# Wider runs in the second pass of a two-layer graph kernel, and its small loads, stores and finals moved to other queues and places

## The reference

```
Ax = A @ x                                            # layer 0, A = adj
x  = layernorm(x + 1.0 - 0.1*x - 0.01*sum(x*Ax, 1))
h  = x                                                # layer 1, adj without its diagonal
support = concat((adj>0)@h, (adj<0)@h)
edge    = gru_cell(support, h, w_ih_e, w_hh_e, ...)
hw      = h @ W
att     = softmax over each row of the logits that adj's signs choose
node    = gru_cell((att*adj) @ hw, h, w_ih_n, w_hh_n, ...)
x  = layernorm(h + diag(adj)*edge + diag(adj)*node)
```

## Time and profile before

| | us |
|---|---|
| median of 3 runs | 1680.99 |
| lowest, highest of them | 1678.02, 1808.76 |
| profiled execution, its own time | 1673.49 |
| its span, first to last instruction | 1671.7 |
| PE, DVE, ACT, POOL busy | 1445.0, 1368.0, 1163.8, 178.0 |

### The profile page before, as it was taken

How to read it: one execution, slowest core, us unless ns; L and a number is a source line. 1 busy time by engine, 2 the same in 40 slices (tenths; PEclk the granted TensorE clock), 3 DMA queues, 4 the chain that set the end, 5 groups by cost and what they waited for, 6 DMA issues and landing times.

```text
span 1671.7 us, 22680 instructions
## 1 busy us (share of the span) xinstructions
PE 1445.0 (86%) x6262; PEld 794.9 (48%) x6262; DVE 1368.0 (82%) x1335; ACT 1163.8 (70%) x1409; POOL 178.0 (11%) x226
## 2 busy tenths in 40 slices
PE   7987878887888888558998899899999899999995
PEld 6655656555555555224444444444444444444442
DVE  5999899898989898647878877887788788778874
ACT  6987979797979797436666666666566666666662
POOL 2000000000001010201101111110111011111100
PEclk9999999999999999779999999999999999999996
DMA  9999999999999999999999999999999999999980
GB/s 264 418 421 422 410 422 409 421 410 421 411 421 413 419 413 419 233 200 333 303 288 306 292 293 296 308 288 291 299 305 298 299 302 295 297 300 310 293 215 11
DMA packets 366090, 550.18 MB, mean 329 GB/s; under 512 B 71024, under 2 KB 333184, under 8 KB 333296
## 3 DMA queue, kind: packets, MB, share of 16 engines
q1 hardware_dynamic: 190672, 408.49, 70.5%
q10 hardware_dynamic: 174976, 141.05, 33.1%
q0 software_dynamic: 416, 0.36, 0.1%
HBM read 545.66 MB, written 4.19 MB: 329 GB/s over the span
## 4 chain that ended last, share of the span: by engine, by line
DMA 30%; issue 21%; ACTq 15%; DVE 15%; PE 9%; ACT 7%; SPq 2%; DVEq 1%; POOL 0%; POOLq 0%
DMA ring<-in_adj 18%; ACTq L247 12%; DMA h_rows<-final 11%; DVE at L806 7%; DVE ps L610 5%; ACT mask L932 5%; PE ps L572 5%; SPq L247 2%; PE ps L1033 2%; ACTq L950 1%; PE ps L539 1%; ACTq L946 1%; PE ps L1045 1%; ACTq L989 0%; ACT final L970 0%
## 5 line engine op out<-in xcount | busy, mean ns | idle before, releaser
L932 ACT ACTIVATE mask<-at 128x2048 fp32r<-128x2048 uint32 x256 | 489.4, 1913 | 281.2 <-DVE at L806 189.6
L572 PE MATMUL ps<-mask,parts 128*128 128x512 f32 x2048 | 552.0, 413 | 101.9 <-DVE ps L610 68.2
L610 DVE SCALAR_TENSOR_TENSOR ps<-ring,ps 128x2048 f32<-128x2048 f32 x256 | 584.3, 2301 | 55.3 <-PE ps L572 34.8
L806 DVE STREAM_TRANSPOSE at<-ring 128x2048 f32<-128x2048 f32 x256 | 577.8, 2290 | 43.6 <-POOL ring L719 37.9
L1033 PE MATMUL ps<-at,hk 128*64 128x512 f32 x2048 | 495.6, 620 | 79.7 <-DVE final L813 42.3
L506 ACT ACTIVATE at<-ring 128x2048 bf16<-128x2048 f32 x256 | 488.7, 1909 | 97.0 <-DMA ring<-in_adj 52.5
L572 PEld LDWEIGHTS ps<-mask,parts 128*128 128x128 f32 x2048 | 374.9, 193 | 278.8 <-DVE ps L610 203.8
L1033 PEld LDWEIGHTS ps<-at,hk 128*64 128x64 f32 x2048 | 148.7, 141 | 346.1 <-issue 250.8
L1045 PE MATMUL ps<-mask,parts 128*128 128x512 f32 x1024 | 270.2, 405 | 13.6 <-ACT final L959 12.9
L1045 PEld LDWEIGHTS ps<-mask,parts 128*128 128x128 f32 x1024 | 182.1, 188 | 152.1 <-issue 73.4
L719 POOL TENSOR_TENSOR ring<-ring,not_diag 128x256 f32<-128x256 f32 x128 | 93.8, 733 | 715.0 <-DMA ring<-in_adj 715.0
(11 more groups left out here) (152 smaller groups left out, 645.4 us busy)
## 6 DMA issues: line engine op xcount, KB each, us to landing
ring<-in_adj SPq DMA_DIRECT2D x256, 1024.0 KB, 16.2
ring<-in_adj SPq DMA_DIRECT2D x264, 512.0 KB, 10.7
ring<-in_adj ACTq DMA_DIRECT2D x248, 512.0 KB, 14.3
stage<-h_rows ACTq DMA_DIRECT2D x16, 128.0 KB, 16.3
nat<-h_rows ACTq DMA_DIRECT2D x16, 128.0 KB, 15.8
out<-final ACTq DMA_DIRECT2D x16, 128.0 KB, 15.4
h_rows<-final ACTq DMA_DIRECT2D x7, 256.0 KB, 22.7
hk<-h_rows ACTq DMA_DIRECT2D x7, 256.0 KB, 23.9
```

The lines of the kernel that those rows point to most:

```text
L572: last = nc.tensor.matmul(ps[:, 4 * (n % 2) + i, :], pair[:, t % 2, e, :], x2[:, cols], start=e == 0, stop=e == 1)
L610: nc.vector.scalar_tensor_tensor(out=gram, in0=ring[:, i % RING, :], scalar=1.0, in1=gram, op0=ALU.mult, op1=ALU.mult, accum_out=flat[:, b ...
L806: nc.vector.transpose(b["at"][:, half % 4, :, :].rearrange("p c (f q) -> p f c q", q=Q), raw[:, :, HC * part:HC * part + HC, :]).then_inc( ...
L932: nc.scalar.activation(b["mask"][:, half % MS, :, :].rearrange("p c i -> p (c i)"), b["at"][:, half % 4, :, :].rearrange("p c i -> p (c i) ...
```

## The change

- **Units.** UC goes from 8 to 16 and a unit takes 256 rows (`RH` = 8 row groups of 32) by 512 columns of each quarter. It is still 2 MB, in runs of 2 KB. Two units side by side in rows (`v` even and odd) feed four halves. A half is now 8 chunks by 256 rows; a turn fills half of the rows of a *pair* of buffers (`pair_view`), and `sign` goes over the same half. PE's weigh and add therefore wait for both halves of their pair, and a turn waits for the weighs and signs of the whole pair two before. A slot comes free after halves 2 and 3 of every four (`freed`), and is used again five halves later.
- **h loaded once a block.** `nat` is gone. POOL loads `stage` (`rows`) behind the first `no_diagonal` of the next block, and `residual` adds from it too.
- **Output.** SP stores it, behind the fifth load of the block after the next one.
- **Weighed sum.** ACT copies both parts out of ACC_T (`weighed_copies`); DVE's `weighed_sum` adds two tiles of SBUF. The first weigh waits for the two copies alone.
- **Finals.** Most steps stand one or two halves later (the tables below); `probabilities` is a step by itself; `variance` stands behind the last turn of a block and `result` in front of the second turn of the next one; `turn_h` goes to PE's third pair, behind `small`.
- **Seam.** Of the first four units SP loads quarters 0 and 1, ACT quarters 2 and 3 (`first_unit`). The norm of the eighth group stands as a whole in front of the first turn; POOL takes its power first, then stores the rows and loads them back on its own queue. ACT makes the high part of both halves of h (`high`), POOL the low part of the first (`first_low`). In the first pass `rows_back` stands four strips later.

```diff
-    UC = 8
-    U = C // UC
+    UC = 16
     SLOTS = 4
-    HC = UC // 2
+    HC = 4
+    RH = BANK // Q // 2
+    U = 2 * (C // UC)
...
+def load_unit(eng, b, prefix, k, v, groups=(0, 1, 2, 3)):
+    RH, UC, GQ, slot = b["RH"], b["UC"], b["GQ"], v % b["SLOTS"]
+    wide, rows = v // 2, v % 2
...
+def freed(v):
+    return 4 * (v // 2) + v % 2 - 5
...
+def pair_view(t, pair):
+    at = 2 * (pair % 2)
+    return t[:, at:at + 2, :, :].rearrange("p s c i -> p (s c) i")
...
-            load_unit(sp, b, "f_", 0, u)
+            load_unit(sp, b, "f_", 0, u, (0, 1))
...
-            if grp and i == 20:
-                rows_back(act, b, grp - 1)
+            if grp and i == 24:
+                act.wait_ge(b["s_scr"], 16 * grp)
+                rows_back(act, b, grp - 1, b["s_hk"][(grp - 1) % 2])
+            done = unit - (GROUPS * self.UNITS - RING)
+            if done in (3, 5, 7):
+                self.first_unit(act, done // 2 - 1)
+        self.first_unit(act, b["SLOTS"] - 1)
...
+    def first_unit(self, act, u):
+        strips = self.UNITS * self.b["GROUPS"] - self.b["RING"] + 2 * (u + 1)
+        act.wait_ge(self.s["signs_summed"], strips)
+        act.wait_ge(self.s["gram_free"], 2 + strips)
+        load_unit(act, self.b, "f_", 0, u, (2, 3))
...
+        def block(k, first, old):
+            for u in range(slots if first else 0, U):
+                sp.wait_ge(s["turned"], k * (2 * U) + freed(u))
                 load_unit(sp, b, "f_", k, u, (0, 1))
+                if old is not None and u == slots:
+                    store(old)
...
+        def rows(k):
+            pool.wait_ge(s["rows_used"], k + 1)
+            pool.dma_start(b["stage"][:, :, :], b["scratch"][bass.ds(k * BANK, BANK), :].rearrange(
+                "(b p) d -> p b d", p=P)).then_inc(s["staged_loaded"], 16)
+        def block(k, prev):
             for u in range(self.U):
                 no_diagonal(nc, pool, b, "f_", k, u).then_inc(s["diagonal_out"], 1)
+                if prev is None and u == 0:
+                    self.first.first_low(pool)
+                if prev is None and u == 1:
+                    pool.wait_ge(b["s_scr_last"], 16)
+                    rows_back(pool, b, last, b["s_hk_last"])
+                if prev is not None and u == 0:
+                    rows(prev)
+        self.first.last_power(pool)
+        store_rows(pool, b, self.first.s["ln_done"], last, b["s_scr_last"])
+        block(0, None)
...
         with pool.Fori(1, self.K) as k:
-            block(k, False)
+            block(k, k - 1)
             power(k - 1)
...
             if not (first and half < 4):
-                dve.wait_ge(s["weighed_done"], n - 3)
-                dve.wait_ge(s["mask_ready"], n - 3)
+                dve.wait_ge(s["weighed_done"], n - rows - 2)
+                dve.wait_ge(s["mask_ready"], n - rows - 2)
...
-            dve.wait_ge(s["weighed_low_copied"], k + 1)
-            nc.vector.tensor_tensor(out=wsum[hi, :], in0=ps[hi, ACC_T, :], in1=lows[hi, :],
+            dve.wait_ge(s["weighed_copied"], 2 * k + 2)
+            nc.vector.tensor_tensor(out=wsum[hi, :], in0=wsum[hi, :], in1=lows[hi, :],
...
-        AT = {3: (weighed_sum,), 4: (added_sum,), 6: (softmax, probabilities), 8: (scale,), 10: (reset,), 11: (update,),
-              14: (residual,), 15: (variance,), 16: (result,)}
-        SEAM = {1: self.first.last_mean, 2: self.first.last_variance, 3: self.first.last_rows, 8: self.first.second_low}
+        AT = {4: (added_sum,), 5: (weighed_sum,), 6: (softmax,), 7: (probabilities,), 10: (scale,), 12: (reset,),
+              13: (update,), 15: (residual,), 16: (variance,)}
+        SEAM = {0: (self.first.last_mean, self.first.last_variance, self.first.last_rows), 8: (self.first.second_low,)}
...
+                if old is not None and half == 1:
+                    result(old)
...
-                act.wait_ge(s["added_done"], n - MS + 1)
+                act.wait_ge(s["added_done"], n - half % 2 - 2)
...
-            u = half // 2 + SLOTS
-            if half % 2 == 1 and (u < U or not last):
+            u = 2 * (half // 4 + 2) + half % 2
+            if half % 4 >= 2 and (u < U or not last):
                 load_unit(act, b, "f_", k + u // U, u % U, (2, 3))
...
-            nc.scalar.copy(b["lows"][hi, :], ps[lo, ACC_T, :]).then_inc(s["weighed_low_copied"], 1)
+            nc.scalar.copy(b["lows"][hi, :], ps[lo, ACC_T, :]).then_inc(s["weighed_copied"], 1)
+            nc.scalar.copy(b["wsum"][0][hi, :], ps[hi, ACC_T, :]).then_inc(s["weighed_copied"], 1)
...
-        AT = {1: (weighed_low, rows), 2: (added_low,), 5: (exps,), 6: (state_in,), 9: (gates,), 10: (new,), 16: (store,)}
+        AT = {1: (weighed_copies,), 2: (added_low,), 6: (exps,), 7: (state_in,), 11: (gates,), 12: (new,)}
...
-                pe.wait_ge(s["weighed_low_copied"], k)
-                pe.wait_ge(s["weighed_summed"], k)
+                pe.wait_ge(s["weighed_copied"], 2 * k)
...
-            pe.wait_ge(s["turned"], k * H + half + 1)
+            pe.wait_ge(s["turned"], k * H + half - half % 2 + 2)
...
-            pe.wait_ge(s["mask_ready"], k * H + half + 1)
+            pe.wait_ge(s["mask_ready"], k * H + half - half % 2 + 2)
...
-        AT = {0: turn_h, 1: small, 2: spread, 3: gates, 5: back}
+        AT = {1: (small,), 2: (turn_h,), 3: (spread,), 4: (gates,), 6: (back,)}
```

More of the change, by code:

```diff
@@ L744, in sync, with store @@
     def sync(self, sp):
-        b, s, U = self.b, self.s, self.U
+        b, s, U, K = self.b, self.s, self.U, self.K
         slots = b["SLOTS"]
[L747 to L751, removed]
-                rows_back(sp, b, last)
-            sp.wait_ge(s["turned"], 2 * (u + 1 - slots))
-            load_unit(sp, b, "f_", 0, u, (0, 1))
-        with sp.Fori(1, self.K) as k:
-            for u in range(U):
-                sp.wait_ge(s["turned"], k * (2 * U) + 2 * (u + 1 - slots))
-                load_unit(sp, b, "f_", k, u, (0, 1))
+        def store(k):
+            sp.wait_ge(s["result_ready"], k + 1)
+            sp.dma_start(b["out"][bass.ds(k * BANK, BANK), :].rearrange("(b p) d -> p b d", p=P),
+                         b["yo"]).then_inc(s["stored"], 16)
+        def block(k, first, old):
+            for u in range(slots if first else 0, U):
+                sp.wait_ge(s["turned"], k * (2 * U) + freed(u))
+                load_unit(sp, b, "f_", k, u, (0, 1))
+                if old is not None and u == slots:
+                    store(old)
+        block(0, True, None)
+        block(1, False, None)
+        with sp.Fori(2, K) as k:
+            block(k, False, k - 2)
+        store(K - 2)
+        store(K - 1)
+        sp.wait_ge(s["stored"], 16 * (K + 1))
     def gpsimd(self, pool):
@@ L901, in block @@
                 if k is not None and half < H:
-                    turn(k, half, first)
+                    turn(k, half, prev is None)
             assert c is None or c.n == CHAIN, c.n
@@ L998, in block @@
                         step(prev)
-                if k is not None and half == 7:
-                    if first:
-                        self.first.second_high(act)
-                    staged_rows(k, first)
+                if first and half in (0, 7):
+                    self.first.high(act, 1 if half else 0)
                 if k is not None and half < H:
@@ L1095, in back @@
             last.then_inc(s["turned_back"], 1)
-        AT = {0: turn_h, 1: small, 2: spread, 3: gates, 5: back}
+        AT = {1: (small,), 2: (turn_h,), 3: (spread,), 4: (gates,), 6: (back,)}
         def block(k, first, prev):
             for pair in range(H // 2):
-                if prev is not None and pair in AT:
-                    AT[pair](prev)
+                for step in AT.get(pair, ()) if prev is not None else ():
+                    step(prev)
                 if k is not None:
```

144 lines of the change are left out of this document (68 added, 76 removed).

## The result

The changed kernel takes 1626.24 us (median of four runs, 1620.43 to 1627.82), the kernel before 1681.35 beside it; the ratio is 0.9672 with an interval of 0.9638 to 0.9707. The forecast was 1628. The profiled execution took 1620.43, its span is 1618.8 where it was 1671.7: 52.9 less.

The account below looks back on a forecast made before the run. PE paces a block (57.7 us, floor 52.9, 4.8 of stalls), and the seam between passes is the other big loss. Seam 26 plus blocks 27 make 53 less than 1681: 1628 us, range 1598 to 1662 (own range 1615 to 1645).

Parts of the forecast that it names:

- The walk's parts: Block's seam, walked from the fifth pair's weigh: floor 52.9 plus waits of 1.75 and 0.7 give a 55.4 us period.
- the first turn 1.85 late for GpSimd: Block's seam: POOL's power and the next `no_diagonal` follow `variance`, so the next block's first turn starts 1.85 us later.
- the weigh's wait 1.75: Start of a block: PE waits 1.75 us for ACT's two copies before the first weigh, where it waited 2.83.
- the add's 0.7: Start of a block: the first add may start at 25.9, the weigh ends at 25.2, so another 0.7 us.
- TensorE's floor: PE's block without stalls: 42.5 plus last pair 5.62, first weigh 3.65 and `turn_h` 1.09, giving 52.9 us.
- The slow first weigh: First weigh of a block still slow in half of the blocks: 0.4 us on average, raising the period to 55.8.
- a sign that it is wrong: In the blocks: DVE waiting for POOL at other turns, because units are late or POOL's issue is long, would refute the forecast.
- `weighed_sum` moves off the path altogether: Block's seam: DVE's `weighed_sum` no longer lies on the path; said with the single load of h, without a size.
- The bound for a landing as on SyncE's queue: Seam: if h's store and load each take 20.9 us, h lands at 737 and the gain of 22 shrinks to 5.
- the lower bound for the 2 KB runs: Loads: 2 KB runs move between 349 GB/s, shown with 1 KB, and 422, shown with 8 KB.
- with a pair of quarters on each queue the same runs come at 349: Seam: SP alone loads quarters at 210 GB/s; two queues with two quarters each bring the same runs at 349.
- The slower rival: POOL's issue of h's load, over 1.3 us, delays the second turn in 15 blocks; up to 1743 us, chance 0.05.

Follow-up runs that it names:

- variance_early: Changed kernel with VectorE computing a block's variance before the block's last turn, not after it: 1597.57 us, 0.954 of the kernel before; repeated on another chip, 1601.71 us.
- h_by_sp: Changed kernel with the last group's h stored and read back by SyncE's queue in place of GpSimd's: 1634.37 us, 0.969 of the kernel before.
- runs_1k: Changed kernel with each load of a quarter issued as two loads of half its columns, so runs are 1 KB: 1635.16 us, 0.971 of the kernel before.
- power_later: Changed kernel with GpSimd's power moved behind the diagonal of the next block's first unit and the load of h: 1613.14 us, 0.963 of the kernel before.
- copies_first: Changed kernel with ScalarE's two copies of the weighed sum ahead of the next block's first sign: 1619.83 us, 0.969 of the kernel before.
- changed_again: The changed kernel, unaltered, run again beside three others to see how much repeats: 1625.55 us, 0.966 of the kernel before.

## Why the prediction was right, point by point

**The block.** Forecast 1.9 less a block and 27 in all; measured 1.96 and 27.4. The walk's parts: the first turn 1.85 late for GpSimd, measured 2.02; the weigh's wait 1.75, measured 2.11; the add's 0.7, measured 0.40; together 2.45, measured 2.51. variance_early shows the link by removing it: 2.0 a block. TensorE's floor, 52.9, was 0.3 too high (55.09 - 2.51 is 52.6). The slow first weigh, taken as half of the blocks, came in three of 14, in another execution in eight. That the period came out at 55.75, where 55.8 was forecast, is in part luck: 55.09, 0.27 for three slow weighs, and 0.4 that nobody counted. Blocks 1 and 2 are 56.58 and 59.30 long; in the second TensorE's gates wait 2.62 for `scale`, which stands behind a turn that waits 6.72 for its unit. The forecast had named such waits as a sign that it is wrong. From block 3 on VectorE still waits 1 to 3 us for a unit in most blocks, and the blocks are not longer for it.

**What the forecast valued too low.** "`weighed_sum` moves off the path altogether" had no price of its own. Undone it costs 43 us of the span (1661.8 against 1618.8), more than all that the blocks gained: the late first turn is bearable only because two copies of 0.6 and not three turns and a sum stand between it and the weigh. With the longer pause the half clock came in every block.

**The seam.** Forecast 26 less with the ninth half at 727.6; measured 25.1 and 729.47. Up to the ninth half it was 20.0 and not 22, from there to block 1 5.1 and not 4: the two errors half cancel. The rate was over 330 as said, and the step of the first pass cost nothing that shows (last gram 688.14 against 687.24, and 686.78 to 689.48 in the other executions). h came back in time: 8.0 for the store. The bound for a landing as on SyncE's queue, a gain of 5 instead of 22, is what h_by_sp shows (12.5 lost instead of 17).

**The step that failed** is the lower bound for the 2 KB runs, "349, shown with 1 KB", and with it "with a pair of quarters on each queue the same runs come at 349". The 349 of the earlier trace rows was seen in one window after the seam, with units asked for a few at a time; at the seam's beginning, with four units asked for one behind the other, 1 KB runs give 232 to 268. So the two queues alone would not have brought the rate over 330: 6.0 to 9.7 of the seam's 25.1 need the 2 KB. The sum came out right because the change has both, and the forecast, which priced the longer runs at nothing, priced the queues as if they did it alone. Undone one at a time, queues, h's way and runs cost 16.7 + 12.5 + 9.7 = 38.9 (35.2 without the 3.7 of the doubled loads), more than the 25.1 that all of them gained: their delays overlap, and the parts don't add up.

**The slower rival.** GpSimd's issues took 0.82 to 1.01, not 0.61. In the blocks the 1.3 of slack held and no turn waits for them. At the seam the store's 1.01 stands in front of the first diagonal, and the first turn, which waited 2.10 for it, is later by the 0.4 that the forecast left out.

**Two transfers at once.** The Trainium skill, SBUF — State Buffer, "Can I just issue two DMAs to hit both halves?", gives 6% more for two transfers. With fixed quarters on two queues the seam moves 352 to 374 instead of 215 to 217, so the measurement decides against it here. Its "Door 1: The DMA port swizzle", with about 218 GB/s for 32 partitions, fits the 215 of one queue.

## What to carry to other kernels

The engine named at the end of a wait is only its last link: price each link by walking the chain, and look what waits next; here the copies were worth 0.26 a block and the variance, further up the same chain, 2.0. When a small step is moved behind the last big one of a loop, ask what it covered, and put it in front if another engine's work hangs on it. A rate seen in one window need not hold in another stage: in runs_1k the same loads came at 347 and at 232 to 268.

## What the runs showed of the hardware that was not expected

- TensorE's clock after a pause. Where the first weigh waits 1.08 (power_later) or 1.16 (copies_first), it took 3.65 in every block whose row is whole. At 1.96 to 2.68 (changed) it was slow in three of 14, at 2.10 to 2.61 (changed_again) in eight of 14, at 4.26 in all 14, with a granted clock of 0.50 behind the pause. The pause alone doesn't decide it: after the longest one of the changed kernel, 2.68, it took 3.65.
- Loads into 32 partitions each: 352 to 374 GB/s with two quarters fixed to each queue and 2 KB runs, 232 to 268 with 1 KB runs, 215 to 217 on one queue, 212 to 279 with whole units on two queues, all at the seam. In the blocks 1 KB and 2 KB runs gave the same 55.05 to 55.12 us.
- A 256 KB store beside these loads: the load back could be issued 8.0 us after it on GpSimd's queue, 22.0 on SyncE's.
